# One head group's outputs get a second buffer, and the step list of a Fourier-attention stage is written anew

## What is computed

```python
q, k, v = (x @ W.T + b, in 16 heads of 32)
feature(h) = concat([cos(h @ proj / sqrt(32)), sin(h @ proj / sqrt(32))]) / sqrt(128)   # 256 per head
kv  = einsum('blhm,blhd->bhmd', feature(k), v)     # a sum over all tokens of the batch
out = einsum('blhm,bhmd->blhd', feature(q), kv) @ Wo.T + bo
x   = layernorm(x + out)
```

## Time and profile before

| | |
|---|---|
| time, median of 3 runs | 1849.26 us (1847.9 to 1851.37) |
| time of the profiled execution | 1849.84 us |
| its span, first to last instruction | 1848.1 us |
| PE busy | 1657.3 us, 90% of the span |
| DVE busy | 1311.1 us, 71% |
| ACT busy | 1149.4 us, 62% |
| POOL busy | 711.3 us, 38% |
| mean granted clock of TensorE | 0.956 of full speed |
| end of `attention` | 1314.0 us |

### The profile page before, as it was taken

How to read it: one execution, slowest core, us unless ns; L and a number is a source line. 1 busy time by engine, 2 the same in 40 slices (tenths; PEclk the granted TensorE clock), 3 DMA queues, 4 the chain that set the end, 5 groups by cost and what they waited for, 6 DMA issues and landing times. The chain is left out here.

```text
span 1848.1 us, 31958 instructions
## 1 busy us (share of the span) xinstructions
PE 1657.3 (90%) x12210; PEld 1175.4 (64%) x12210; DVE 1311.1 (71%) x1821; ACT 1149.4 (62%) x1510; POOL 711.3 (38%) x641
## 2 busy tenths in 40 slices
PE   4998998998999899899899989965698898899995
PEld 3755765675676577567467657733466776677784
DVE  4575766757667666765766767687588878888885
ACT  2595776777577577667857757755145554555564
POOL 3031212404313130340431313053286767777776
PEclk9999999999999999999999999987799999999998
DMA  4100202202011020220201102013211212222201
GB/s 152 47 24 1 70 2 69 69 1 70 25 46 44 27 70 1 69 69 1 70 24 47 42 29 70 1 46 111 80 49 56 79 63 75 74 68 74 69 35 57
DMA packets 49102, 95.87 MB, mean 52 GB/s; under 512 B 3472, under 2 KB 3792, under 8 KB 48976
## 3 DMA queue, kind: packets, MB, share of 16 engines
q1 hardware_dynamic: 38864, 76.29, 13.1%
q10 hardware_dynamic: 10112, 17.69, 2.6%
HBM read 60.38 MB, written 33.59 MB: 51 GB/s over the span
## 5 line engine op out<-in xcount | busy, mean ns | idle before, releaser
L698 DVE SCALAR_TENSOR_TENSOR feat<-feat,phases 128x1024 f32<-128x1024 f32 x256 | 301.0, 1217 | 197.2 <-ACT feat L595 197.2
L595 ACT ACTIVATE feat<-phases 128x1024 f32<-128x1024 f32 x256 | 248.3, 1023 | 217.6 <-PE phases L457 123.7
L602 ACT ACTIVATE feat<-feat 128x1024 f32<-128x1024 f32 x256 | 271.5, 1061 | 84.9 <-DVE feat L698 76.0
L385 POOL TENSOR_TENSOR ln<-moments,eps 128x4 f32<-128x4 f32 x16 | 3.2, 202 | 741.4 <-DVE moments L747 741.4
L608 ACT ACTIVATE feat<-feat 128x1024 f32<-128x1024 f32 x256 | 256.9, 1047 | 17.0 <-DVE feat L705 16.9
L705 DVE TENSOR_SCALAR feat<-feat 128x1024 int32<-128x1024 int32 x256 | 213.9, 840 | 47.9 <-ACT feat L602 47.7
L446 PE MATMUL bank<-wo_hi,att_hi 128*128 128x512 f32 x256 | 110.9, 433 | 51.3 <-DVE att_lo L731 43.0
L544 PE MATMUL kv_sum<-feat,kv_cols 128*32 128x512 f32 x1024 | 126.4, 612 | 8.6 <-ACT feat L608 8.6
L372 POOL TENSOR_TENSOR res<-res,bo_all 128x512 f32<-128x512 f32 x64 | 85.2, 1359 | 118.9 <-DMA res<-x 118.4
L446 PE MATMUL bank<-xt_hi,win_hi 128*128 128x512 f32 x256 | 109.2, 427 | 19.4 <-POOL xt_lo L363 19.4
L518 PE MATMUL kv_sum<-feat,v 128*32 128x256 f32 x2048 | 123.8, 382 | 0.0
(11 more groups left out here) (178 smaller groups left out, 4156.6 us busy)
## 6 DMA issues: line engine op xcount, KB each, us to landing
normed<-res SPq DMA_DIRECT2D x32, 513.0 KB, 4.7
xt_raw<-xT SPq DMA_DIRECT2D x16, 1024.0 KB, 6.2
res<-x SPq DMA_DIRECT2D x32, 512.0 KB, 4.2
xs<-normed SPq DMA_DIRECT2D x24, 513.0 KB, 4.1
out<-xs ACTq DMA_DIRECT2D x24, 512.0 KB, 2.8
feat<-normed SPq DMA_DIRECT2D x8, 513.0 KB, 3.8
out<-feat ACTq DMA_DIRECT2D x8, 512.0 KB, 2.8
fold<-ctx SPq DMA_DIRECT2D x8, 256.0 KB, 3.8
```

The lines of the kernel that those rows point to most:

```text
L595: act.activation(feat[2 * (w % 2) + p][:, 0, :], phases[:, 2 * p:2 * p + 2, :].rearrange("p h n -> p (h n)"), ACT.Identity, bias=ROUND).th ...
L602: act.activation(f[:, 1, :], f[:, 0, :], ACT.Sin, scale=-TWO_PI).then_inc(sin_done, 1)
L698: dve.scalar_tensor_tensor(f[:, 0, :], f[:, 0, :], ROUND, phases[:, 2 * p:2 * p + 2, :].rearrange("p h n -> p (h n)"), ALU.subtract, ALU.s ...
```

## The change

- **Second buffer.** Out(12), the first group of chunk 1, writes to `spare_hi` and `spare_lo` in `kept.fold` instead of group 0 of `att_hi` and `att_lo`. It may so run while W(0, *) still read those. The context rows of part two, which used `fold`, go to `xt_raw`.
- **Pair matmuls behind the phases.** kv(w - 1) or out(w - 1) now stands first under w, ahead of the sine and the products; only under 10, 13 and 14 W products stand before it.
- **Respread.** W(0, *) stand two and two under 13 and 14, no longer right behind out(11); W(1, *) under 7 to 10, before under 4 to 7; V one each under 11, 12, 15 and 0 to 4. Under 5 and 6 a single product is left. The normalisation of chunk 1 moves from 9 to 11. The loop starts at Q(1, 1) under 11.
- **Tail.** `win` is prepared at the tail's start from `v[0]`, whose load is issued in the last batch; the `wf` steps move, and `add_bias` on POOL follows the dequantisation.
- **POOL** splits the input before `powers`.
- **Part two** begins with another order of its first slot, and POOL's wait for `bf_all` moves from its start to the first use.

```diff
-START = 10
+START = 11
@@ def attention_steps
-        12: [sin(12), Q(1, 2), cos(12), out(11), W(0, 0), W(0, 1)],
-        13: [sin(13), W(0, 2), W(0, 3), cos(13), Q(1, 3), out(12)],
+        12: [out(11), sin(12), Q(1, 2), V(0, 1), cos(12)],
+        13: [sin(13), W(0, 0), W(0, 1), cos(13), out(12), Q(1, 3)],
+        5: [kv(4), sin(5), K(1, 3), cos(5)],
+        6: [kv(5), save(0), sin(6), Q(0, 0), cos(6)],
+        7: [kv(6), sin(7), Q(0, 1), W(1, 0), cos(7)],
+        8: [kv(7), save(1), sin(8), Q(0, 2), W(1, 1), cos(8), turned(0)],
+        9: [out(8), sin(9), Q(0, 3), turned(1), W(1, 2), cos(9)],
+        10: [sin(10), W(1, 3), cos(10), out(9), stats(1), Q(1, 0)],
@@ first batch
-        1: [sin(1), K(0, 3), cos(1), V(0, 2), V(0, 3), V(1, 0), kv(0)],
-        2: [sin(2), K(1, 0), cos(2), V(1, 1), V(1, 2), kv(1)],
+        1: [sin(1), K(0, 3), cos(1), V(0, 2), V(0, 3), kv(0)],
+        2: [kv(1), sin(2), K(1, 0), cos(2), V(1, 0), V(1, 1)],
+        3: [kv(2), sin(3), K(1, 1), cos(3), V(1, 2)],
+        4: [kv(3), sin(4), K(1, 2), V(1, 3), cos(4)],
@@ tail
+        12: [out(11), sin(12), Q(1, 2), wf(1), cos(12), wf(2)],
+        13: [sin(13), W(0, 0), W(0, 1), cos(13), out(12), Q(1, 3)],
+        14: [sin(14), W(0, 2), W(0, 3), cos(14), out(13), stats(0), wf(3), wf(4)],
+        15: [out(14), sin(15), cos(15), norm(0, 0), norm(0, 1), out(15), wf(5), W(1, 0), W(1, 1), ("ends",), W(1, 2), W(1, 3),
+             stats(1), norm(1, 0), norm(1, 1)],
+    tail = [("win",), Q(1, 1), wf(0), cos(11)]
@@ def attention
+        spare_hi, spare_lo = (kept.fold[:, n * CHUNK:(n + 1) * CHUNK].bitcast(F32R) for n in range(2))
-        wf_grid, wround, wq, win_stage = kept.xt_raw, v[0][:], v[1][:], in_rows(feat[2])
+        wf_grid, wround, wq, win_stage = kept.xt_raw, v[0][:], v[1][:], v[0]
+        def att_parts(c, g):
+            return (spare_hi, spare_lo) if c == 1 and g == 0 else (att_hi[:, g, :], att_lo[:, g, :])
@@ SP, last batch
+                    sp.wait_ge(feat_used, KPAIRS * i + GROUPS)
+                    sp.dma_start(win_stage[:], WinT.rearrange("(k p) o -> p k o", p=P)).then_inc(win_in, 16)
@@ POOL, batch
                 if mode == "tail":
                     round_weight()
+                    powers(2 * i - 2)
                     dequantise_weight()
+                    add_bias(2 * i - 1)
+                    powers(2 * i - 1)
...
+                split(i, 1, i, mode)
+                powers(2 * i - 2)
+                add_bias(2 * i - 1)
                 if mode != "last":
+                    split(i + 1, 0, i, mode)
+                powers(2 * i - 1)
                 add_bias(2 * i)
@@ PE, out
-                        freed(order.of(mode, ("kvt", g // 2), s))
                         if w < KPAIRS + len(out_part):
+                            freed(order.place(mode, ("kvt", w - KPAIRS)))
@@ part two, first slot
-            [("select",), ("turn", 0), ("patch",), ("means",), ("count",), ("choose",), ("turn", 1),
-             ("norms",), ("table",)],
+            [("select",), ("turn", 0), ("patch",), ("count",), ("table",), ("choose",), ("turn", 1), ("means",), ("norms",)],
@@ part two, POOL
+                            if mode == "first" and k == 0:
+                                pool.wait_ge(bias_in, 16)
...
-            pool.wait_ge(bias_in, 16)
```

More of the change, by code:

```diff
@@ L70, in place @@
         if back:
-            assert self.first[step] == self.full[step] - self.left
-            return self.full[step] - self.left - self.n
+            return self.first[step] - self.n
         if mode == "first":
@@ L86, in ring @@
     def ring(self, mode, step, depth):
-        assert self.n % depth == 0 and self.left % depth == 0
+        assert self.n % depth == 0
         return self.place(mode, step) % depth
@@ L132, in attention_steps @@
         steps += [("phase", w)] + after[w]
+    turn = steps.index(Q(1, 1))
     own = {K(0, 0), K(0, 1)} | {V(0, t) for t in range(TPC)}
-    ahead = steps[:steps.index(("phase", 0))]
-    left = {x for x in ahead if x not in own} | {out(15), stats(1)} | {norm(1, h) for h in range(2)} | {W(1, t) for t in range(TPC)}
+    left = {x for x in steps[turn:] if x not in own} | {out(15), stats(1)} | {norm(1, h) for h in range(2)} | {W(1, t) for t in range(TPC)}
+    steps = steps[turn:] + steps[:turn]
@@ L144, in attention_steps @@
         first += [("phase", w)] + after[w]
-    first += [x for x in steps[steps.index(("phase", 3)):] if x not in left]
+    first += [x for x in steps[steps.index(("phase", 5)):] if x not in left]
     after = {
-        10: [wf(0), sin(10), Q(1, 0), wf(1), cos(10), out(9)],
-        11: [sin(11), Q(1, 1), wf(2), cos(11), out(10)],
-        12: [sin(12), Q(1, 2), cos(12), out(11), W(0, 0), W(0, 1)],
-        13: [sin(13), W(0, 2), W(0, 3), cos(13), Q(1, 3), stats(0), out(12)],
-        14: [sin(14), wf(3), cos(14), out(13), norm(0, 0), norm(0, 1)],
-        15: [sin(15), cos(15), out(14), wf(4), out(15), ("win",), W(1, 0), W(1, 1), W(1, 2), W(1, 3), stats(1), wf(5), ("ends",),
-             norm(1, 0), norm(1, 1)],
-    }
@@ L156, in attention_steps @@
-    tail = []
-    for w in range(START, PAIRS_A):
+        12: [out(11), sin(12), Q(1, 2), wf(1), cos(12), wf(2)],
[3 more added lines that the diff above has]
+             stats(1), norm(1, 0), norm(1, 1)],
+    }
+    tail = [("win",), Q(1, 1), wf(0), cos(11)]
@@ L158, in attention_steps @@
+    for w in range(START + 1, PAIRS_A):
         tail += [("phase", w)] + after[w]
@@ L349, in _, with split @@
         def _(pool):
-            def split(i, c, mode):
-                k = 2 * i + c
+            def split(own, c, i, mode):
+                k = 2 * own + c
                 pool.wait_ge(xt_loaded, 16 * (k + 1))
-                if mode != "first":
-                    last_query = ("q", c, GROUPS - 1)
-                    pool.wait_ge(product_done, order.at(i, mode, last_query, back=last_query not in left) + 1)
-                if mode != "first" or c != 0:
+                fresh = isinstance(own, int) and own == 0
+                if not fresh:
+                    pool.wait_ge(product_done, order.at(i, mode, ("q", c, GROUPS - 1)) + 1)
+                if not fresh or c != 0:
                     for n in range(KD):
@@ L411, in batch @@
                 if mode == "first":
-                    split(0, 0, mode)
-                    split(0, 1, mode)
-                    split(1, 0, "loop")
+                    split(0, 0, 0, mode)
+                    split(0, 1, 0, mode)
+                    split(1, 0, 0, mode)
                     add_bias(0)
@@ L554, in batch @@
                         rows = slice(t * P, t * P + P)
-                        product(b[:], lambda m: att_hi[:, m, rows], lambda m: att_lo[:, m, rows],
+                        product(b[:], lambda m: att_parts(c, m)[0][:, rows], lambda m: att_parts(c, m)[1][:, rows],
                                 lambda m: whi["o"][:, m, :], lambda m: wlo["o"][:, m, :]).then_inc(product_done, 1)
@@ L619, in batch @@
                         act.wait_ge(out_done, out_order.at(i, mode, s) + 1)
-                        act.activation(att_hi[:, w % GROUPS, :], out_part[w % len(out_part)], ACT.Identity).then_inc(hi_ready, 1)
+                        act.activation(att_parts(w // GROUPS - CHUNKS, w % GROUPS)[0], out_part[w % len(out_part)], ACT.Identity).then_inc(hi_ready, 1)
                     elif kind == "win":
```

49 lines of the change are left out of this document (18 added, 31 removed).

## The result

The changed kernel takes 1824.99 us in the median of four runs (1821.03 to 1834.3), against 1850.32 of the kernel before beside it: a ratio of 0.9869 (95% interval 0.9826 to 0.9912). It is faster by 25 us (16 to 32 by that interval).

A forecast was written before the change was run, and what follows sets the result against it. PE's work, idle time and lower-clock loss were taken as the bound. Batches -43.8, first batch +3.4, tail -6.1 and part two -3.1 sum to -49.6: 1849.8 becomes 1800 us, four in five from 1768 to 1826.

The forecast's parts named there:

- What is removed: In the loop, W(0, 0)'s wait and those at phases 10 to 12 go: 11 us of idle and clock loss a batch.
- PE's own work: PE's matmul work at full clock in one loop batch, put at 143.2 us from timeline rows and the batch windows.
- The four added waits: New PE waits a batch: 1.4 at kv(5), 1.4 at kv(6), 0.75 at out(8), 1.25 us at W(1, 2).
- Together 4.8 us a batch: Sum of the waits that the new order adds in each loop batch, none over 1.4 us; bounds 0 and 10.
- the batch of 148.0: Loop batch forecast: 143.2 of work plus 4.8 of waits, instead of 154.26; 43.8 us less over seven.
- By that row my four waits cost no clock: In the loop, the short added waits were to leave PE's clock up, as in the first batch: no cost.
- The rival that I gave 0.13: The clock still falls once or twice a loop batch: 12 to 24 us in all, 1812 to 1824; chance 0.13.
- the rule of the Trainium skill that spoke against the change: Frequent short idle times between groups of matmuls make PE's clock oscillate and cost throughput; weighed against the added waits.
- The row of the first batch: Profile before: PE waits 1.42 and 1.70 us in the first batch, yet the granted clock is 1.00.
- First batch: Products 5 to 10 are single and ACT waits for each, 0.75 us in six steps: 3.4 us longer.
- Tail: From phase 11 to part two, earlier `win` and reordered waits: 96.5 against 102.56, 6.1 us less, to 8 either way.
- Part two: POOL no longer waits early for the bias, so the table's matmul starts sooner: 3.1 us less, between 0 and 3.4.

The follow-up runs named there:

- e6: The changed kernel with kv(5), kv(6) behind their products, the transposes at the front of phases 8 and 9, and TensorE's loop written out: 1772.96 us, 0.9572 of before.
- e3: The changed kernel with the pairs kv(5) and kv(6) moved behind the products Q(0,0) and Q(0,1): 1801.96 us, 0.9731 of the kernel before.
- e4: The changed kernel with the transposes kvt(0) and kvt(1) moved to the front of phases 8 and 9: 1814.36 us, 0.98 of the kernel before.
- e2: The kernel before the change, with only TensorE's loop over the batches written out as straight code: 1856.6 us, 1.0035 of the kernel before.
- e1: The changed kernel with only TensorE's loop over the seven batches written out as straight code: 1812.75 us, 0.9795 of the kernel before.
- e9: The changed kernel with kv(5), kv(6) behind their products and TensorE's loop written out, transposes not moved: 1788.09 us, 0.9655 of the kernel before.
- e5: The changed kernel with kv(5), kv(6) behind their products and the transposes at the front of phases 8 and 9, loop kept: 1790.35 us, 0.9653 of before.
- e10: The kernel of e6 with a first batch whose pairs stand behind their products, as before the change: 1771.35 us, 0.9579 of the kernel before.
- e11: The kernel of e6 with W(0,0) and W(0,1) of the tail ahead of sin(13): 1773.84 us, 0.9584 of the kernel before.
- e7: The kernel before with only part two's edits, the first slot's order and POOL's later wait for the bias: 1849.4 us, 0.998 of before.

## Why the prediction was right or wrong, point by point

- **What is removed: right.** W(0, 0) waits for nothing, the 43.0 us for att_lo are gone in the loop, and PE's own work is 143.25 us a batch (e6), forecast 143.2. The phases' and products' rows alone had given 142.8; that 143.2 was taken between this and the 143 to 144 of the windows is in part luck.
- **The four added waits: right in place and releaser, a little too long.** 1.18, 1.18, 0.84 and 1.13 are 4.3 us a batch for 4.8. e3 and e4 took them away pair by pair, and got their sum.
- **"Together 4.8 us a batch", and the batch of 148.0: the step that failed.** I listed the four places where a wait is added and left out a fifth, the loop's edge on PE, which the sum so has at nothing. The change moves the start of the loop from phase 10, where PE had to let ACT and DVE catch up, to Q(1, 1), where everything is ready. The 2 us that the trace of before shows there under stack_lo were the edge itself (e2), and cost nothing, since they came back as a wait one phase later when it was taken away. After the change they cost 1.7 to 2.0 us at six places, 10.8 us. Two of the six falls of the clock hang on them as well, 3.4 us. With PE's loop written out a batch without a fall takes 147.90 (e1): the 148.0 would have stood, though by luck to the tenth, as waits taken 0.5 us too long and PE's busy time taken 0.4 us too short (143.60 in e1) make up for each other. The Trainium skill has the rule, in "Runtime: NRT & Kernel Launch", section "Instruction fetch mechanics": a taken branch whose target is out of the sequencer's current window has to fetch it first. It gives no time for it, the trace agrees as far as it goes, and I hadn't weighed it. The Trainium skill's "Advanced Engine Details and Errata", section "Control Flow Timing", gives a branch 0.05 to 0.11 us, and by that the sum would have been within 1 us of the one that I made; the measurement says 1.7 to 2.0 us at the edge. That fetching is the cause isn't shown by any run here; that the loop construct is, e1 shows.
- **"By that row my four waits cost no clock": wrong in the batches.** Six falls of 1.7 us cost 10.2 us, four of them at the 1.18 us waits. The rival that I gave 0.13 forecast 12 to 24 us for it. So the rule of the Trainium skill that spoke against the change ("TensorE: Matmul & The Clock Gate", "A second HAM failure mode: psum-queue depth-cycling") was the better guide, though not for all of my four waits: those of 0.8 and 1.1 us alone are followed by no fall in seven batches (e9), the 1.18 ones by three (e1), the edges alone by five in six (e5). The row of the first batch was too little to price it by, and the trace of before said otherwise elsewhere. The idle 2.03 us of the earlier trace rows are followed by a fall within 2 us of the phase's start, and so are at once the edge's 2.02 us in the batch shown under e2 and 2.08 in the next one, while the edge's other four are not:

```profile
441.60:444.80 3.20, 3.20 (x9) 2.52 (x8) 1.38 (x3) 3.20 (x5) 1.13 (x1) 0.50 0.75 249
...
588.40:591.70 3.30, 3.30 (x11) 2.42 (x8) 3.30 (x5) 2.11 (x3) 3.22 (x4) 0.50 0.18 68
```

- **First batch: +6.9 instead of +3.4.** Right in sign, and mis-sized. The waits in the changed kernel's first batch are six from 98 us on, of 1.18 to 1.77 and 8.5 us together, with one fall of the clock at the longest; I had 0.75 a step. That ACT sets the pace there is not settled (e10).
- **Tail: -3.2 instead of -6.1.** Waits of 3.78, 9.48 and 1.90 stand where 4.0, 9.3 and 2.4 were placed, but out(15) waits 9.03 and not 14, and 4.08 for the dequantised weight, which I hadn't listed. A long wait on PE is no price by itself here: e11 takes 8 us from one and wins nothing.
- **Part two: -7.4 instead of -3.1.** The start is right, 3.2 us (e7 has it alone). The other 4 come without the edits (e7): 2.0 of them are PE's busy time at another clock and the rest idle time, and both differ between kernels whose second part is the same.

In sum: 10.8 us for the edge, 10.2 for the clock and 2.6 of PE's busy time over 143.2 a batch, less 3.3 of overrated waits (0.47 in each of seven), give the 20.3 that the seven batches lack; the first batch adds 3.5 and the tail 2.9, and part two gives 4.3 back: 22.4, as 49.6 less 27.2.

## What to carry to other kernels

Treat the edge of a loop as an instruction with a price on each engine, and see what covers it: when an order is rotated, the edge moves with it, and the bound engine's edge belongs where that engine waits anyway, or the loop is written out. Put the consumer of a late operand behind a product and not ahead of it, and what another engine must copy ahead of that engine's long work: these two moves and the loop written out turned 150.9 us a batch into 143.25, without any less work. A short wait on TensorE can cost about twice its length or more, since some bring a fall of the clock with them (1.7 us behind waits of 1.2 to 2.3 here); price both.

## What the runs showed of the hardware that I had not expected

- PE stands idle for 1.7 to 2.3 us at a branch back (six times in each kernel that keeps the loop), in a loop whose body has some 1250 matmul rows in the profile's windows, and the profile gives it to "issue", or, in the kernel before, mostly to stack_lo, which e2 shows was not what held it.
- Each fall of the clock in the loop costs 1.7 us. Whether one follows isn't set by the length of the wait alone: waits of 0.8 and 1.1 us alone had none in seven batches (e9), those of 1.7 to 2.3 at the edge had five in six in e5, two in six in the changed kernel and one in six in e3, and a wait of 2.5 in the first batch of e9 had none. What decides it stays open.
- With no wait at all, PE kept the higher clock for 860 us on end, six batches of 143.25 us to the hundredth.
- The same second part, with the same instructions, takes 522.5 to 530.6 us from its first table_sum on in different kernels (e6 and e11), 6.9 of the 8.2 us by PE's busy time at another clock. That is more than a small edit wins.
